# A graph network kernel on one core: the weight work around the edge loop in another order, and the second layer's bias row made behind the loop

## The reference

```python
# block 1: weighted, normalised adjacency; two linear maps and a leaky relu in each of two layers
A = zeros((1024, 1024)).at[src, dst].add(edge_weight);  deg = sum(A, axis=1);  dinv = deg ** -0.5
A_norm = dinv[:, None] * A * dinv[None, :];  h = x
for l in range(2):
    h = A_norm @ h
    h = h @ W_gcn[l] + b_gcn[l]
    h = leaky_relu(h @ W_mlp[l] + b_mlp[l], 0.01)
x = layernorm(x + h)
# block 2: the same edges unweighted, with self loops, symmetric norm, two layers with W1, b1, W2, b2
x = layernorm(x + gcn2(relu(gcn1(x))))
```

## Time and profile before

| | before |
|---|---|
| median of 3 runs (lowest, highest) | 335.67 us (334.77, 335.86) |
| profiled execution, its own time | 335.47 us |
| its span from first to last instruction | 333.6 us |
| PE busy | 314.5 us, 94% |
| DVE busy | 189.0 us, 57% |
| ACT busy | 122.0 us, 37% |
| POOL busy | 49.9 us, 15% |
| mean granted TensorE clock | 0.997 |

### The profile page before, as it was taken

The page is one execution under the profiler, slowest core; times in us unless marked ns, Lnnn a source line. Parts: engine busy times, 40 slices in busy tenths (PEclk is TensorE's granted clock), DMA queues, the critical chain, the costliest instruction groups (busy, mean ns, idle before and its releaser), DMA issues.

```text
span 333.6 us, 4919 instructions
## 1 busy us (share of the span) xinstructions
PE 314.5 (94%) x1977; PEld 259.7 (78%) x1977; DVE 189.0 (57%) x333; ACT 122.0 (37%) x253; POOL 49.9 (15%) x54
## 2 busy tenths in 40 slices
PE   2878999998999999999999999999999999999993
PEld 1767786876788888888888888888888888888882
DVE  6998999714544611165643457675953444225664
ACT  3637889546434401134432013233702444220000
POOL 2100000001005970100000011121680000001111
PEclk9999999999999999999999999999999999999998
DMA  6270000700000000000700000006100000000121
GB/s 211 66 254 2 3 2 0 249 6 2 3 0 1 2 0 0 2 0 0 238 15 0 2 0 0 0 4 226 61 2 0 0 0 2 0 4 33 63 84 73
DMA packets 8590, 13.43 MB, mean 40 GB/s; under 512 B 1906, under 2 KB 2290, under 8 KB 8564
## 3 DMA queue, kind: packets, MB, share of 16 engines
q1 hardware_dynamic: 8564, 13.05, 11.6%
HBM read 10.95 MB, written 2.10 MB: 39 GB/s over the span
## 4 chain that ended last, share of the span: by engine, by line
PE 88%; DVE 7%; issue 2%; ACT 1%; DMA 1%; POOLq 0%; POOL 0%; SPq 0%; ACTq 0%
PE psum L650 75%; PE psum L708 6%; PE psum L636 3%; DVE hot L1004 2%; PE psum L755 1%; DVE sel L996 1%; PE psum L830 1%; DVE hot L999 1%; PE psum L692 1%; DVE wm_low L1089 1%; DVE wgt_low L1076 1%; PE psum L714 1%; DMA src_i<-in_src 1%; PE psum L864 1%; ACT hot L455 0%
## 5 line engine op out<-in xcount | busy, mean ns | idle before, releaser
L441 POOL TENSOR_TENSOR small<-small 128x1 f32<-128x1 f32 x16 | 11.9, 742 | 161.6 <-DVE small L1272 161.6
L708 PE MATMUL psum<-hot,sel 128*128 128x96 bf16 x512 | 32.3, 215 | 2.1 <-DVE hot L1004 1.3
L708 PEld LDWEIGHTS psum<-hot,sel 128*128 128x128 bf16 x512 | 28.4, 101 | 7.5 <-issue 6.9
L650 PE MATMUL psum<-at_high,x_high 128*128 128x512 f32 x64 | 25.8, 403 | 0.6 <-DVE x_low L1200 0.6
L1076 DVE SCALAR_TENSOR_TENSOR y_low<-psum,small,y_high 128x512 fp32r<-128x512 f32 x16 | 11.9, 750 | 24.2 <-ACT y_high L455 24.2
L650 PE MATMUL psum<-at_low,x_high 128*128 128x512 f32 x64 | 25.1, 392 | 0.0
L650 PE MATMUL psum<-y_high,at_high 128*128 128x512 f32 x64 | 25.0, 391 | 0.0
L650 PE MATMUL psum<-cnt,x_high 128*128 128x512 f32 x64 | 25.0, 390 | 0.0
L650 PE MATMUL psum<-at_high,x_low 128*128 128x512 f32 x64 | 25.0, 390 | 0.0
L650 PE MATMUL psum<-cnt,x_low 128*128 128x512 f32 x64 | 25.0, 390 | 0.0
L650 PE MATMUL psum<-y_low,at_high 128*128 128x512 f32 x64 | 24.9, 390 | 0.0
(11 more groups left out here) (185 smaller groups left out, 755.3 us busy)
## 6 DMA issues: line engine op xcount, KB each, us to landing
wg_raw<-in_L_gnn_W_gcn SPq DMA_DIRECT2D x2, 1024.0 KB, 5.5
x_raw<-in_x SPq DMA_DIRECT2D x1, 2048.0 KB, 10.3
xs<-in_x SPq DMA_DIRECT2D x1, 2048.0 KB, 9.3
w_raw<-in_L_gnn_W SPq DMA_DIRECT2D x2, 1024.0 KB, 8.1
out<-xs SPq DMA_DIRECT2D x8, 256.0 KB, 2.0
wm_raw<-in_L_gnn_W_mlp SPq DMA_DIRECT2D x1, 1024.0 KB, 8.2
wm_next<-in_L_gnn_W_mlp SPq DMA_DIRECT2D x1, 1024.0 KB, 8.8
bias_bc<-in_L_gnn_b SPq DMA_DIRECT2D x1, 256.0 KB, 8.2
```

The lines of the kernel that those rows point to most:

```text
L441: pool.tensor_tensor(r[:, 1:2], r[:, 0:1], power[:, 0:1], ALU.pow).then_inc(rstd_ready, 1)
L650: ins = pe.matmul(dest, s, m, start=first and n == 0, stop=end and n == len(pairs) - 1, skip_group_check=True)
L708: ins = pe.matmul(sums[1 if k == 0 else 0], stationary, moving, start=False, stop=False, skip_group_check=True)
```

## The change

It has four parts. (a) The order: the four blocks of `wgt0` stand ahead of chunk 0 (a stop called FIRST), and so do the full clears of regions 0 and 1; `wc0`, `bias0`, `biasb0` and `wgt1` stand behind earlier chunks than before; `wc1` is cut into other portions. (b) DVE's written order follows that, and `SHARED` keeps only batch 7, so DVE makes k = 4 of batches 4 and 5 itself. (c) `bias1` is done behind the transposes of adjacency blocks 0 to 2, ahead of the first `g1_a` step, and `biasb1` behind that step; both take banks from the same ring, and their rows lie in a tile of their own, `next_rows`. (d) `x_raw` is read in eight pieces of 256 KB, and each waits for the one before it; this begins after `biasb0` and the 16 `scale_columns` of batch 7.

```diff
-    SHARED = {4: {21: 6, 27: 10}, 5: {40: 16}, 7: {66: 8, 73: 8}}
+    SHARED = {7: {66: 8, 73: 8}}
...
+        next_rows = at("next_rows", B2, [3, D], F32)
...
-        fillers = {3: [("wgt0", 0, 0, KD)], 10: [("wgt0", 1, 0, KD), ("wgt0", 2, 0, KD)], 15: [("wgt0", 3, 0, KD)],
-                   27: [("wc0", 0, 0, KD)], 31: [("wc0", 1, 0, KD), ("prep", 4, 0, KD)], 34: [("wc0", 2, 0, 2)],
-                   40: [("wc0", 2, 2, KD), ("wc0", 3, 0, 2)], 47: [("wc0", 3, 2, KD), ("bias0", 0, 0, KD)],
-                   53: [("biasb0", 0, 0, KD), ("wgt1", 0, 0, KD), ("wgt1", 1, 0, KD)],
-                   60: [("wgt1", 2, 0, KD), ("wgt1", 3, 0, KD)], 66: [("bias1", 0, 0, KD)],
-                   73: [("biasb1", 0, 0, KD), ("wc1", 0, 0, 2)], 79: [("wc1", 0, 2, KD)], 86: [("wc1", 1, 0, 2)],
-                   92: [("wc1", 1, 2, KD)], 99: [("wc1", 2, 0, 2)], 105: [("wc1", 2, 2, 3)], 112: [("wc1", 2, 3, KD)],
-                   CH - 1: [("wc1", 3, 0, KD)]}
+        FIRST = -1
+        fillers = {FIRST: [("wgt0", i, 0, KD) for i in range(KD)],
+                   7: [("wc0", 0, 0, KD)], 8: [("wc0", 1, 0, KD)], 15: [("wc0", 2, 0, 2)], 21: [("wc0", 2, 2, KD)],
+                   27: [("wc0", 3, 0, KD)], 31: [("bias0", 0, 0, KD), ("prep", 4, 0, KD)],
+                   34: [("biasb0", 0, 0, KD), ("wgt1", 0, 0, KD), ("wgt1", 1, 0, KD)],
+                   40: [("wgt1", 2, 0, KD), ("wgt1", 3, 0, KD)], 60: [("wc1", 0, 0, KD)], 63: [("wc1", 1, 0, 2)],
+                   73: [("wc1", 1, 2, 3)], 79: [("wc1", 1, 3, KD)], 86: [("wc1", 2, 0, 2)],
+                   92: [("wc1", 2, 2, 3)], 99: [("wc1", 2, 3, KD), ("wc1", 3, 0, 1)], 105: [("wc1", 3, 1, 2)],
+                   CH - 1: [("wc1", 3, 2, KD)]}
...
-        loads = {15: [16], 31: [32], 47: [48, 64], 73: [80], 86: [96], 105: [112]}
+        loads = {15: [16], 27: [32], 31: [48], 60: [64], 63: [80], 86: [96], 99: [112]}
...
         for j in range(NB):
             in_ring("at", j, FILL)
+            if j in (2, 3):
+                in_ring("bias1" if j == 2 else "biasb1", 0, FILL)
...
             sp.wait_ge(done["biasb0"], 1)
-            sp.dma_start(bias_rows[2:3, :], bm[1:2, :]).then_inc(bm_in, 16)
-            sp.wait_ge(done["biasb1"], 1)
             sp.wait_ge(scaled, G * len(SHARED))
-            sp.dma_start(x_raw[:], x.rearrange(by_k, p=P)).then_inc(x_in, 16)
+
+            for j in range(NB):
+                if j:
+                    sp.wait_ge(x_in, 16 * j)
+                sp.dma_start(x_raw[:, j, :], x[j * P:(j + 1) * P, :]).then_inc(x_in, 16)
+
+            sp.wait_ge(region_done, 1 + closing.index(99))
+            sp.dma_start(next_rows[2:3, :], bm[1:2, :]).then_inc(bm_in, 16)
...
-                if c == 3:
-                    split_wm(0, range(3))
-                if c == closing[0]:
-                    split_wm(0, range(3, KD))
-                if c == 47:
+                if c == FIRST:
+                    split_wm(0, range(KD))
+                if c == 31:
                     split_wm(1, range(KD))
...
                 if j == 0:
-                    act.wait_ge(x_in, 16)
+                    act.wait_ge(x_in, 16 * NB)
...
                 if j + 1 < NB:
                     upper_at("at", 0, j + 1)
+                if j in (1, 2):
+                    upper_fill("bias1" if j == 1 else "biasb1", 0)
...
             pe.wait_ge(consts, 12)
+            for r in range(2):
+                clear(r)
             pe.wait_ge(off_ready, 1)
             pe.wait_ge(column_ready, 1)
+            for name, i, k0, k1 in fillers[FIRST]:
+                filler(name, i, k0, k1)
             load_offsets(0)
...
             for j in range(3):
                 turn_adjacency("at", 0, j)
+            filler("bias1", 0, 0, KD)
             pe.wait_ge(evacuated, copies(NR - 1))
...
                 if j + 3 < NB:
                     turn_adjacency("at", 0, j + 3)
+                if j == 0:
+                    filler("biasb1", 0, 0, KD)
```

More of the change, by code:

```diff
@@ L515, in upper_fill @@
                 elif name.startswith("bias"):
-                    if name == "bias1":
-                        act.wait_ge(done["biasb0"], 1)
-                    copy(bias_rows[0:2, :], bank(name)[0:2, :]).then_inc(taken[name], 1)
+                    copy((next_rows if name == "bias1" else bias_rows)[0:2, :], bank(name)[0:2, :])\
+                        .then_inc(taken[name], 1)
                 else:
@@ L747, in filler @@
                     else:
-                        ins = pe.matmul(b, ones3[:], bias_rows[:], start=True, stop=True)
+                        ins = pe.matmul(b, ones3[:], next_rows[:], start=True, stop=True)
                 else:
@@ L771, in _ @@
                 for r in range(NR):
-                    if opening[r] == c:
+                    if r >= 2 and opening[r] == c:
                         clear(r)
@@ L1096, in _ @@
             make_all(1)
-            make_all(2)
+            lower_fill("wgt0", 0)
+            make(2, 0)
+            lower_fill("wgt0", 1)
+            lower_fill("wgt0", 2)
+            make(2, 1)
+            lower_fill("wgt0", 3)
+            lower_wm(0)
+            for k in range(2, 5):
+                make(2, k)
             make(3, 0)
-            lower_fill("wgt0", 0)
+            lower_fill("wc0", 0)
             for k in range(1, 5):
                 make(3, k)
[L1102 to L1105, removed]
+            lower_fill("wc0", 1)
             make_all(4)
+            lower_fill("wc0", 2)
             check_windows()
@@ L1109, in _ @@
             make_hw()
-            lower_fill("wc0", 0)
-            lower_fill("wc0", 1)
-            make_all(5)
+            lower_fill("wc0", 3)
             take_flag()
[L1114 to L1119, removed]
+            make(5, 0)
+            make(5, 1)
             for i in range(2):
                 lower_fill("wgt1", i)
-            for k in range(1, 5):
-                make(7, k)
+            for k in range(2, 5):
+                make(5, k)
+            add_ends(0)
             for i in range(2, KD):
                 lower_fill("wgt1", i)
+            lower_wm(1)
+            make_all(6)
             add_ends(1)
+            make_all(7)
+            lower_fill("wc1", 0)
             make_all(8)
-            make(9, 0)
-            make(9, 1)
             add_ends(2)
-            for k in range(2, 5):
-                make(9, k)
-            lower_fill("wc1", 0)
+            make_all(9)
             lower_fill("wc1", 1)
```

## The result

The changed kernel is slower: 338.95 us (median of 4 runs, 337.75 to 339.29) against 335.22 us (4 runs, 334.70 to 335.86), a ratio of 1.0104 [1.0070, 1.0138]. A second set gave 338.17 us (5 runs) against 335.13 us (27 runs), 1.0089 [1.0075, 1.0104]. The forecast, 337.4 us, has the right sign and is 0.8 us under the one median and 1.6 under the other. It was reckoned from an own time of before of 335.47 us, which is above both medians of before; as a difference it said 1.9 us, and 3.7 and 3.0 were measured.

What follows compares the result with a forecast made beforehand. PE was taken as the bound, DVE nearly as full in the middle. The walk gave +1.0 us to the loop's end, then -0.15 and +1.05 behind it: +1.9 on 335.47, so 337.4 us, range 335.0 to 339.6.

Steps and rivals of the forecast that it cites:

- The start: Up to the 35 degree matmuls: `wc0 0` starts at 15.4, they end at 35.4; wins 3.5 us.
- The middle: Chunks 47 to 86: PE waits for DVE and ACT and at stops without filler; chunk 86 ends at 62.3, before 60.65.
- The end of the loop: From chunk 86 to the loop's last chunk: 17.1 us, with 0.9 new wait at stop 112; ends at 79.4.
- The bias row: Behind the loop: some 1.0 of `bias1`'s 1.86 us on the path, first product at 85.0; `biasb1` uncovered, 1.05 us.
- The rival by which the row is hidden anyway: Behind the loop: `at_low` 0 comes 1 us earlier than put, time 336.4 us, inside the range; no chance of its own.
- the transfer: Eight x pieces from 60.2 us at 2.5 each, all landed at 80.2, needed at 82.2, 83.2 still free: no cost.
- the x pieces come late: Rival at x_high of block 0: decides from 2.87 us a piece; at 3.3 the time is 340.8 us; chance 0.08.
- end step: Behind the loop: `bias1` leads to the first product at 85.0; wrong if `bias1` ends before x_low of block 0.
- The clock's rival: Rival at `wc0 0`: after the wait at 14 us products run slowly, time up to 340.3 us; chance 0.05.
- The win of the start: Rival at stops 47 to 83: waits vanish, 334.6 us or 331.1 if all go; chance 0.14 faster, 0.20 no difference.
- the 6.35 us of new waits forecast: PE waits in the loop: 0.6 + 1.6 + 0.8 + 0.8 + 0.9 + 0.3 + 0.45 + 0.9 us.
- no difference: Case at stops 47 to 83: from 0.9 to 2.9 us of waits gone, time as before; chance 0.20.

Runs made afterwards that it cites:

- the first combined kernel: Changed kernel with x in one transfer, no `SHARED`, `bias1` behind chunk 66 and `biasb1` behind 112, DVE's order kept: 335.01 us, 0.9991 of the kernel before.
- the best kernel: The first combined kernel with `prep` ahead of `bias0`, window check after `make(3, 0)`, first region ends ahead of two low parts of W_gcn[1]: 333.76 us, 0.9966.
- the busy wait: Changed kernel with five extra PE matmuls of 512 zero columns ahead of the clear before chunk 50: 336.97 us, 1.0069 of the kernel before.
- the ends first: Changed kernel with DVE adding the first group of region ends ahead of the last three parts of batch 5: 337.19 us, 1.0076 of the kernel before.
- the early flag: Changed kernel with `prep` 4 behind chunk 18, DVE's window check ahead of `low(wc0 0)` and its flag ahead of batch 4: 338.11 us, 1.0082.

## Why the prediction was right, and which term was too small

**The start was right.** `wc0 0` starts at 15.67 (15.4 said), behind an idle PE; the degree matmuls end at 35.68 (35.4). The win was 3.5 by the sum and 3.2 measured.

**The middle was right in place and nearly in size.** Chunk 48 waited until 42.37 (42.2), the clear before 50 until 44.41 (44.2), released by ACT's copy behind DVE's ends. The waits from there on were 0.1 to 0.2 us shorter than walked, since two or three chunks cover a little more than I took, but for that at chunk 80 (as walked) and that before chunk 57 (0.17 for 0.8). There the half clock shows: the chunks ahead of this clear took longer and the wait shrank by as much, so that it comes 2.45 us behind the clear before chunk 50, in this profile as in those with a whole clock (44.75 and 47.20 with one x transfer). Only the slow chunks behind it cost, and that is the 0.9. Chunk 86 ended at 63.33 (62.3): without the clock's 0.9 it would have been 62.4.

**The end of the loop** came at 79.5 (79.4). From chunk 86 on it was 16.2 us, 0.9 less than the 17.1 of the sum. So two errors cancelled here: the clock, and a last part of the loop made too long. Before had two pauses in it (0.39 and 0.24 us, put down to issue) that the changed kernel has not, and the wait at the empty stop is 0.75 instead of 0.9.

**The bias row was right.** `bias1` stood on the path up to the first product, at 85.41 (85.0), and `biasb1` cost 1.0 to 1.15 behind it (1.05). The rival by which the row is hidden anyway has fallen, by these figures and by the run with the row alone behind the loop.

**The term that was too small is the transfer.** The prediction took the x pieces as hidden, with all landed at 80.2 and a deciding price of 2.87 us a piece. Its 2.5 us is nearly what most pieces take (2.6 in the median), but it had no room for single long ones: 3.2 us in the first profile, 4.59 and 3.28 in the second. They also start at 61.1 to 61.2, not 60.2. So the last lands at 82.7 in one profile and at 84.2 in the other, where it costs 0.7 us; the mean of the eight is (84.2 - 61.1) / 8 = 2.89 us there. The rival "the x pieces come late", with a chance of 0.08, holds beside the forecast in part of the executions, and by the prediction's own sign its end step fails in the second profile: `bias1` ends before x_low does, and PE waits 0.50 us for x_low. One x transfer takes 1.0 us off the median, of which the two profiles give 0.7 to the pieces. The second profile closes the account: it is 2.8 us over before, 1.73 at the first product (85.87 instead of 84.14; 0.85 forecast) and 1.08 behind it (1.05 forecast). The rest, up to the 3.0 us between the medians, is that the profiled execution of before was a slow one among its runs (335.47 against a median of 335.13).

The Trainium skill (DMA: Bandwidth & Descriptors, Anatomy of one DMA) gives a transfer that GpSimd issues about 2.0 us of fixed cost and its bytes at 436 GB/s besides; that is an estimate of 2.6 us for 256 KB. The pieces here are issued by SyncE, and their median agrees (2.6 us), while the output's transfers of the same size took 2.0 in all, so that row does not bear out the fixed cost as the prediction has it.

**The clock's rival was in the wrong place.** I put it at the wait of 14 us. There nothing came of it in the changed kernel: the first `wc0` blocks took 2.98 and 2.81 us. The slow pace came at the waits of 42 to 44 us, which I had counted myself. In three profiles of other kernels a slow pace did stand there, but ahead of the wait and not brought by it, and chunks 0 to 7 then ended at 15.3 to 15.8 us, not before 14.

**The win of the start did not survive**, for the reason given: of the 6.35 us of new waits forecast, PE's timeline shows 4.66 (0.64 + 1.46 + 0.17 + 0.65 + 0.68 + 0.31 + 0.75), about 0.3 more stand before the clear at 62.29 (chunk 80 from 61.39 and two more chunks end at 62.0), and 0.9 went to the clock. With batch 7's columns on DVE, 1.0 to 1.3 us of these waits and the late pieces are gone, and the kernel is within 0.3% of before, where the rival puts "no difference".

The repairs add up: the first combined kernel was expected at 335.0 and gave 335.01. That the whole forecast came so near has luck in it: the clock's 0.9 us, which it did not have, was made up by the last part of the loop.

## What to carry to other kernels

Work moved into the idle time of the first engine wins only as long as the next engine isn't late for it: here PE's early 3.2 us were paid back as waits for DVE's and ACT's, as DVE had hardly any reserve in the middle. Before a stretch is moved forward, walk the second engine's list as well, and leave some piece of work at every stop where PE must wait for a copy. A row of transfers that wait for each other adds up its slow ones, so it needs room behind it and not only a median that fits: in the profiles the same eight pieces cost nothing from 58.7 us on and up to 0.7 from 61.1.

## What the runs showed of the hardware

**In these profiles the granted clock falls to half at most once before the end of the loop, and its place varies.** In the changed kernel's profile PE was idle for 0.64 and 1.46 us with two chunks between them, worked 1.0 us at full pace, and from 45.4 to 48.75 us the granted clock was 0.51, that is TensorE's lower level of 1.2 GHz; four chunk matmuls take 0.38 us there and 0.21 elsewhere. The same waits in the kernel with one x transfer had a clock of 1.00. What differs is the start. There, in the kernel without `SHARED` and in the best kernel the first 32 chunk matmuls took 3.0 us; the chain of waits of the best kernel, then the same piece of the changed one:

```profile
12.25 3.00 PE psum L714 x32
```

```profile
12.25 1.67 PE psum L717 x32
```

In these first matmuls the granted clock reads 0.50 in the best kernel, but 1.00 in the other two, though the pace is the same; so a row of 1.00 is no proof of the full pace there. In none of the three profiles does the clock fall between there and the first product. Of the eight profiles of the changed kernel and its variants in which these matmuls took 1.67 us, it fell between 44 and 50 us in five and at 38 in one. In the other two, the busy wait and the ends first, it did not fall at all; these are the two in which one of the two waits near 43 us was filled or merged into the other. That is two profiles and no rule: with the early flag one of the two waits was only 0.28 us, and the clock fell all the same. The slow start costs nothing where PE must wait for `wm_low` anyway: in the best kernel `wc0 0` starts at 15.67 either way. Without `SHARED` it cost some 0.8: the transposes of W_gcn were slow too, so DVE waited 0.46 us for ACT's high part and `wc0 0` started late, at 16.22, and its first two products still took 0.9 us in place of 0.5.

The Trainium skill (TensorE: Matmul & The Clock Gate, What's actually happening) has 1.2 GHz as the resting level from which activity releases 2.4. The trace agrees on the two levels (0.50 and 1.00). What decides between the two starts stays open: the kernels have the same instructions up to there, or nearly so, and each was profiled once (the changed one twice, both times with the fast start). Open too is why single runs of several kernels (337.42 us with the pieces in the kernel before, 338.89 with the ends first) lie 1.7 to 2.5 us above their median, and the effect of an early flag, since the kernel made for it only moved DVE's lateness.
